# Two shared-key attentions with their q and k stacks loaded by DMA, and narrower causal scores

## The reference

```python
def _L2_xattn_ref(q, k, v):            # q = layernorm(x), k = v = ctx_512
    H, KV = 32, 8; D = E // H; G = H // KV
    qh = q.reshape(b, s, KV, G, D).transpose(0, 2, 3, 1, 4)
    kh = k.reshape(b, s, KV, D).transpose(0, 2, 1, 3)
    vh = v.reshape(b, s, KV, D).transpose(0, 2, 1, 3)
    scores = jnp.einsum('bkgsd,bktd->bkgst', qh, kh) / sqrt(D)
    weights = jax.nn.softmax(scores, axis=-1)
    out = jnp.einsum('bkgst,bktd->bkgsd', weights, vh)
x = x + _L2_xattn_ref(_layernorm(x), ctx_512, ctx_512)
```

## Time and profile before

| what | value |
|---|---|
| median of 3 runs | 4070.13 us (4068.88 to 4073.53) |
| the profiled execution | 4041.53 us |
| its span, first to last instruction | 4039.8 us |
| mean granted TensorE clock | 0.923 of full |
| PE busy | 3451.4 us (85%), 18066 instructions |
| PE weight loads | 2386.6 us (59%) |
| VectorE busy | 2419.2 us (60%) |
| ScalarE busy | 2054.4 us (51%) |
| GpSimd busy | 898.4 us (22%) |
| DMA | 346.47 MB, mean 86 GB/s |

### The profile page before, as it was taken

The page is one execution under the profiler, slowest core; times in us unless marked ns, Lnnn a source line. Parts: engine busy times, 40 slices in busy tenths (PEclk is TensorE's granted clock), DMA queues, the critical chain, the costliest instruction groups (busy, mean ns, idle before and its releaser), DMA issues. The chain is left out here.

```text
span 4039.8 us, 64864 instructions
## 1 busy us (share of the span) xinstructions
PE 3451.4 (85%) x18066; PEld 2386.6 (59%) x18070; DVE 2419.2 (60%) x4267; ACT 2054.4 (51%) x3563; POOL 898.4 (22%) x1818
## 2 busy tenths in 40 slices
PE   4349996899972799839999799899897999989998
PEld 2137775666651688714444367788775444436886
DVE  6964445455543333368888554666466788865665
ACT  5643333355531455427877633566433677774433
POOL 2410001544322100053333130122113333310000
PEclk8669998999986899959999899999998899999999
DMA  3424442400011333320000252577442000002223
GB/s 138 148 99 140 137 136 76 167 0 0 1 52 44 122 107 99 104 83 1 0 0 0 71 177 93 180 240 240 169 140 81 1 0 0 0 9 73 93 93 114
DMA packets 133100, 346.47 MB, mean 86 GB/s; under 512 B 15300, under 2 KB 15428, under 8 KB 132338
## 3 DMA queue, kind: packets, MB, share of 16 engines
q1 hardware_dynamic: 99666, 228.74, 17.5%
q0 software_dynamic: 22480, 96.23, 7.0%
q10 hardware_dynamic: 10864, 20.45, 1.4%
HBM read 274.58 MB, written 68.16 MB: 85 GB/s over the span
## 5 line engine op out<-in xcount | busy, mean ns | idle before, releaser
L1338 DVE TENSOR_REDUCE at_maxima<-psum 128x1 f32<-128x512 f32 (+1 forms) x1280 | 813.5, 661 | 288.8 <-PE psum L1148 134.8
L1309 ACT ACTIVATE at_probs<-psum 128x512 f32<-128x512 f32 (+3 forms) x1280 | 692.8, 570 | 352.1 <-PE psum L1159 200.4
L1144 PE MATMUL psum<-at_kT,at_qT 64*128 64x512 f32 (+2 forms) x1280 | 555.7, 480 | 14.9 <-DVE at_kT L1351 8.8
L1159 PE MATMUL psum<-at_qT_max,at_kT 64*128 64x512 f32 (+4 forms) x1280 | 533.0, 454 | 27.9 <-ACT at_probs L1309 23.3
L1159 PEld LDWEIGHTS psum<-at_qT_max,at_kT 64*128 64x128 f32 (+1 forms) x1280 | 218.3, 186 | 341.8 <-ACT at_probs L1309 294.6
L573 PE MATMUL psum<-f_xT_hi,ffn_w_hi 128*128 x1024 | 405.2, 396 | 9.0 <-DVE f_xT_lo L2050 2.2
L573 PE MATMUL psum<-f_xT_lo,ffn_w_hi 128*128 x1024 | 404.4, 395 | 0.0
L1176 PE MATMUL psum<-at_probs,at_vals 128*32 128x512 f32 (+4 forms) x2560 | 375.7, 578 | 2.1 <-issue 2.1
L1112 PE MATMUL psum<-ident,at_arr 128*128 128x128 f32 x1536 | 255.8, 292 | 97.2 <-POOL at_arr L1015 94.9
L1112 PEld LDWEIGHTS psum<-ident,at_arr 128*128 128x128 f32 x1536 | 169.2, 145 | 200.9 <-POOL at_arr L1015 96.2
L1003 POOL TENSOR_TENSOR at_gap<-ones 128x1 f32<-128x1 f32 x448 | 87.2, 195 | 850.3 <-DVE at_result L1365 600.0
(11 more groups left out here) (379 smaller groups left out, 7264.7 us busy)
## 6 DMA issues: line engine op xcount, KB each, us to landing
ffn_w_raw<-in_stream SPq DMA_DIRECT2D x262, 256.0 KB, 2.8
ffn_w_hi<-quantized SPq DMA_DIRECT2D x66, 512.0 KB, 3.5
ffn_w_hi<-quantized SPq DMA_DIRECT2D x65, 256.0 KB, 3.1
ffn2a_w_raw<-in_shared2a SPq DMA_DIRECT2D x26, 512.0 KB, 3.6
ffn2b_w_raw<-in_shared2b SPq DMA_DIRECT2D x26, 512.0 KB, 3.6
qz_raw<-in_stream SPq DMA_DIRECT2D x17, 768.0 KB, 4.3
quantized<-qz_quant POOLq DMA_DIRECT2D x16, 768.0 KB, 3.5
gathered<-zeros SPq DMA_DIRECT2D x1, 12288.0 KB
```

What stands on the lines that cost most here:

```text
L1144: mm = pe.matmul(bank[:, 0:width], qT[ring % 2][rows_of(h), h // HPS, t * P:(t + 1) * P], kT[ring][rows_of(h), h % 2, 0:width], start=True ...
L1159: mm = pe.matmul(bank[:, 0:S - lo], kT[ring][rows_of(h), h % 2, t * P:(t + 1) * P], qT_max[ring % 2][rows_of(h), h // HPS, lo:S], start=Tr ...
L1309: act.activation(probs[n % RING][:, 0:S - lo], scoreT[n % 2][:, 0:S - lo], ACT.Exp, scale=factor).then_inc(exped, 1)
L1338: dve.tensor_reduce(maxima[:, t, h:h + 1], (score + scoreT)[n % (4 if first else 2)][:, 0:width], AX.X, ALU.max).then_inc(maxed, 1)
```

## The change

1. The shared attentions get a stage of their own, `stage_attend_shared`. The norm now leaves the queries transposed, `xT` (high and low part, features on partitions), by its own transposes on PE into banks 4 to 7. SP spills them to DRAM (`spill`, per batch two DMAs of 1 MB), and `load` builds each group's stacks straight from DRAM: 12 DMAs, six of 64 KB for q and six of 32 KB for k. The keys' high and low parts are spilled to DRAM once, in `stage_keys_values`, by 8 DMAs of 256 KB, whose end ScalarE waits for before it reuses a buffer.
2. Groups go batch by batch (8 key heads of batch 0, then batch 1), where before batches alternated; the host's layout of `ctx_g` follows. The loop holds 8 slots now and runs 3 times.
3. The maxima go a new way: VectorE writes them to a buffer of their own (`split`), one `turn_max` after pair 5 turns them, ScalarE moves 8 rows (`maxT`), and SP puts them into the stacks by 4 DMAs (`put_max`). `turn_results` stands after pair 9. All transposes use one bank.
4. VectorE takes one maximum over two banks (two heads), 8 per group in place of 16; scores have four banks. The matmuls contract over 48 and 50 rows in place of 64.
5. POOL no longer stacks; it copies the values (`keep_values`) in place of VectorE. The clearing at the start goes from POOL to VectorE.
6. Causal scores are P (t + 1) columns wide, and their mask is always 128.

The core of the diff:

```diff
@@ stage_norm
+def stage_norm(k, nm, xT=None, tokens=None, rows=None, joined=None, beside=None, before=None, bank=0):
+            turned_ps = [room.tiles(bank + u) for u in range(TB)]
...
@@ stage_attend, scores and max_tile
-                width = min(S, P * (t + 2 - t % 2)) if causal else S
+                width = P * (t + 1) if causal else S
...
-                    m = 2 * P if t % 2 == 0 else P
-                    mm = pe.matmul(bank[:, t * P:t * P + m], ident16[:, :], mask[:, 0:m], start=False, stop=True, skip_group_check=True)
+                    mm = pe.matmul(bank[:, t * P:(t + 1) * P], ident16[:, :], mask[:, :], start=False, stop=True, skip_group_check=True)
...
@@ stage_attend_shared (new)
+    HD, H, PARTS = HEAD2, 4, 3
+    USED = PARTS * HD
+    HALF = P // 2
+    PAIRS = H * TB
+    SETS = PAIRS // 2
+    RING, SLOTS = 2 * H, 4
+    OW = P // H
+    ROUND = GROUPS // B
+    ROUNDS = (GROUPS - 1 - SLOTS) // ROUND
+    LOADS, PUTS = 2 * PARTS * 2, H
+    LAST, VALUES, MAX, RES = 1, (5, 9, 13), 5, 9
...
+        score, scoreT, res, turn = [room.psum[:, 1024 * m:1024 * m + 1024] for m in range(2)], room.banks[4:6], room.banks[6], room.tiles(7)
...
+        def head_tile(n):
+            return n // (PAIRS // 2), 1 - n % 2, n % (PAIRS // 2) // 2
...
+        @block.vector
+        def _(dve):
+            for r in range(SLOTS):
+                dve.memset(kT[r][:, :].bitcast(F32), -1.0).then_inc(cleared, 1)
+            for r in range(2):
+                dve.memset(vals[r][:, :, :], 0.0).then_inc(consts, 1)
+                dve.memset(split[r][:, :, :, :].bitcast(F32), 0.0).then_inc(consts, 1)
+            dve.wait_ge(consts, 4)
+            for r in range(2):
+                dve.memset(vals[r][:, :, HD:HD + 1], 1.0).then_inc(consts, 1)
+        made, before = queries(room, xT)
+        def spill(sp, b):
+            sp.wait_ge(made, before + TB * (b + 1))
+            part = slice(b * S, (b + 1) * S)
+            for dst, src in zip((q_hi, q_lo), xT):
+                sp.dma_start(dst.rearrange("(c p) t -> p c t", p=P)[:, :, part], src[:, :, part].bitcast(F32)).then_inc(spilled, DMA)
+        @block.sync
+        def _(sp):
+            sp.wait_ge(cleared, SLOTS)
+            def load(place, j):
+                b, n = batch_piece(place, j)
+                r, tokens = place % SLOTS, bass.ds(b * S, S)
+                for par in range(2):
+                    for i, src in enumerate((q_hi, q_lo, q_hi)):
+                        at = HALF * par + HD * i
+                        rows = src[n * H * HD:(n + 1) * H * HD, tokens].rearrange("(jj par d) t -> par d jj t", jj=2, par=2)
+                        sp.dma_start(qT[r][at:at + HD, :, :].bitcast(F32), rows[par]).then_inc(landed[r], DMA)
+                    for i, src in enumerate((k_hi, k_hi, k_lo)):
+                        at = HALF * par + HD * i
+                        sp.dma_start(kT[r][at:at + HD, :].bitcast(F32), src[n * HD:(n + 1) * HD, tokens]).then_inc(landed[r], DMA)
+            def put_max(place, j, g):
+                r = place % SLOTS
+                sp.wait_ge(max_moved, g + 1)
+                for jj in range(2):
+                    for par in range(2):
+                        at = HALF * par + USED
+                        row0 = 2 * (2 * jj + 1 - par)
+                        sp.dma_start(qT[r][at:at + 2, jj, :].bitcast(F32), maxT[place % 2][row0:row0 + 2, :]).then_inc(put[r], DMA)
+            spill(sp, 0)
+            sp.wait_ge(spilled, 2 * DMA)
+            for g in range(SLOTS - 1):
+                load(g, 0)
+            for b in range(1, B):
+                spill(sp, b)
+            put_max(0, 0, 0)
+            sp.wait_ge(spilled, 2 * B * DMA)
+            def slot(s, place, j, ahead):
+                if ahead >= 3:
+                    if not is_first(s):
+                        sp.wait_ge(scoredT, PAIRS * s)
+                    load(place + 3, j)
+                if ahead >= 1:
+                    put_max(place + 1, j, s + 1)
+            all_slots(sp, slot)
...
+            def scores(g, place, j, n):
+                jj, par, t = head_tile(n)
+                r, m = place % SLOTS, n // 2
+                if n == 0:
+                    pe.wait_ge(landed[r], LOADS * DMA * (use(place, j) + 1))
+                if n % 2 == 0:
+                    pe.wait_ge(maxed, SETS * g + m + 1)
+                mm = pe.matmul(score[m % 2][:, 512 * (n % 2):512 * (n % 2) + S], qT[r][half(par, USED), jj, t * P:(t + 1) * P],
+                               kT[r][half(par, USED), :], start=True, stop=True)
+                if n % 2 == 1:
+                    mm.then_inc(scored, 1)
+            def scores_T(g, place, j, n):
+                t, h, r = n // H, n % H, place % SLOTS
+                if n == 0:
+                    pe.wait_ge(put[r], PUTS * DMA * (use(place, j) + 1))
+                pe.wait_ge(exped, PAIRS * g + n + 1)
+                pe.matmul(scoreT[n % 2][:, :], kT[r][half(h % 2, USED + 2), t * P:(t + 1) * P], qT[r][half(h % 2, USED + 2), h // 2, :],
+                          start=True, stop=True).then_inc(scoredT, 1)
...
+            for g in range(2):
+                for n in range(PAIRS):
+                    scores(g, g, 0, n)
+                    if g == 1 and n == MAX:
+                        pe.wait_ge(made, before + N // P)
+                        turn_max(0, 0)
+            def slot(s, place, j, ahead):
+                first = is_first(s)
+                for n in range(PAIRS):
+                    scores_T(s, place, j, n)
+                    if ahead >= 2:
+                        scores(s + 2, place + 2, j, n)
+                    if n == LAST and not first:
+                        results(s - 1, place + 3, TB - 1)
+                    if n in VALUES:
+                        results(s, place, VALUES.index(n))
+                    if n == MAX and ahead >= 1:
+                        pe.wait_ge(max_moved, s + 1)
+                        if not first:
+                            pe.wait_ge(finished, s)
+                        turn_max(s + 1, place + 1)
+                    if n == RES and not first:
+                        pe.wait_ge(res_moved, s)
+                        if ahead >= 1:
+                            pe.wait_ge(max_moved, s + 2)
+                        else:
+                            pe.wait_ge(finished, s)
+                        turn_results()
...
+                for n in range(PAIRS):
+                    act.wait_ge(scoredT, PAIRS * s + n + 1)
+                    act.wait_ge(valued, PAIRS * s + n + 1)
+                    act.activation(probs[n % RING][:, :], scoreT[n % 2][:, :], ACT.Exp, scale=factor).then_inc(exped, 1)
+                    if n == LAST + 1 and not is_first(s):
+                        move_res(s - 1)
+                    if n == MAX + 1 and ahead >= 1:
+                        move_max(s + 1, place + 1, j)
...
+            def max_set(g, m):
+                jj, _, t = head_tile(2 * m)
+                dve.wait_ge(scored, SETS * g + m + 1)
+                dve.tensor_reduce(maxima[:, t, 2 * jj:2 * jj + 2], score[m % 2].rearrange("p (h s) -> p h s", h=2), AX.X, ALU.max).then_inc(maxed, 1)
...
@@ stage_keys_values
+            def batch(b, s):
+                sp.wait_ge(c_lo_made, b + 1)
+                for dst, src in ((k_hi, c_hi), (k_lo, c_lo)):
+                    sp.dma_start(dst[:, bass.ds(b * S, S)], src[s][:, :].bitcast(F32)).then_inc(kept[s], DMA)
...
+                act.wait_ge(kept[s], 2 * DMA * (uses + 1))
@@ lay_out
-        "ctx_g": np.ascontiguousarray(ctx_512.reshape(B, TB, P, 8, HEAD2).transpose(2, 3, 0, 1, 4).reshape(P, GROUPS, TB, HEAD2)),
+        "ctx_g": np.ascontiguousarray(ctx_512.reshape(B, TB, P, 8, HEAD2).transpose(2, 0, 3, 1, 4).reshape(P, GROUPS, TB, HEAD2)),
```

216 lines of the change are left out of this document (176 added, 40 removed).

## The result

| | before | changed |
|---|---|---|
| median | 4070.13 us (7 runs, 4064.8 to 4075.5) | 4081.12 us (7 runs, 4075.2 to 4090.2) |
| ratio, 95% interval | | 1.0029 (1.0017 to 1.0042) |
| span of the profiled execution | 4039.8 us | 4079.3 us |
| mean granted clock | 0.923 | 0.910 |

The change makes the kernel slower, by 0.3%. The forecast was 8.5 us faster; the time is inside its range, the direction is wrong. The page of the changed kernel: engines, then the granted clock by 40 slices.

A forecast was written before the change was run, and what follows sets the result against it. The prediction took a loop of waits between PE and ScalarE to bound the shared attentions' slots. Its terms, -14 - 8.5 + 6 + 3 + 5 = -8.5 us, applied to the median 4070.1, gave 4061.6 us, range 4022 to 4096.

The forecast's parts named there:

- What bounds the kernel: Shared attentions: a loop between PE and ScalarE sets each slot's four quarters (3.10, 3.59, 4.18, 3.69 us), not PE's sum.
- VectorE: In the slots: eight reductions of 1024 at 1.2 us each, at most 12.2 of 14.56 us, not on the path.
- The register instructions: In the shared attentions' loops: one more PE register instruction per second pair, 0.05 us each, +3 us, bounds -11 to +17.
- The causal attention: First attention, 32 slots: four tiles per slot lose 128 columns of score and mask, 0.44 us a slot, -14 us.
- the two ways in: Stretches before the first transposed score: second attention -8.5 us (-12 to -4), third attention +6 us (+2 to +10).
- The slots: Second and third attention: a slot stays 14.56 us, leaving only +3 us in the loops and +5 in the last slots.
- The last slots: End of both shared attentions, from slot 29, with fewer transposes and scores: +0.7 and +1.8 us, +5 for two layers.
- (a): Rival: PE is the bound after all, so fewer transposes shorten the slots: about 3920 or about 4000 us; chance 0.10.
- (b): Rival: the DMAs of a slot land 1 us late in each slot, +60, about 4130 us; chance 0.08.
- (c): Rival: register waits take 0.3 us a slot (+14), ways in at upper bounds (+4.5, +4): about 4084 us; chance 0.11.
- (d): Rival: matmuls of 48 and 50 rows no longer run side by side, +300, about 4370 us; chance 0.01.
- The sum: Whole kernel: -14 - 8.5 + 6 + 3 + 5 = -8.5 us, with bounds of -31 and +21.

The follow-up runs named there:

- act4: The changed kernel with ScalarE's loop of 8 slots written as one of 4 slots, the same instructions executed in the same order; ratio 1.0012 to the kernel before.
- moves_only: The changed kernel with its two ScalarE moves, move_res and move_max, one exponential later each, transposes left in place; ratio 0.9882 to the kernel before.
- place_act4: The changed kernel with turn_max after pair 3, turn_results after 11, move_res after exponential 3, and ScalarE's loop of 4 slots; 3934.6 us, ratio 0.9677.

## Why the prediction was wrong

- **What bounds the kernel: right.** "So a quarter is not PE's sum." A third of PE's transposes stayed, PE's busy time fell by 8 of 50 us, and the slot stayed at 14.5. All four quarters came out within 0.04 us, and the experiments moved three of them by the amount that the loop gives, while 3.10 stayed.
- **VectorE: right.** A reduction of 1024 takes 1.22 us (1.2 taken), and nothing waits for it in the loop.
- **The register instructions: wrong, small.** "I take 0.05 for it": a quarter at full clock lost nothing. In the loops of act4, which no pause or fall disturbs, a slot is 14.51 us against 14.56, so the +3 is -3.
- **The causal attention, the two ways in: right**, -13.4, -7.8 and +5.6 for -14, -8.5 and +6.
- **The slots: the step that failed.** "In the loops PE has one more register instruction for each second pair" is all that I let the new loops cost, with bounds from -11 to +17. Two things were missing, the jump back and the clock, both put at nothing without a reason. The loop body became 8 slots long, which the part on the change says itself; each of its two jumps back in an attention stops ScalarE for 2.0 us. And the earlier trace rows show a full clock at 49.4 of 50 us busy; I carried that clock over to a PE that is busy 41.5. The four pauses with their falls measured 14.6 us, lone falls 7.3, falls in the last slots 13.5. act4 took the first away (1.0012), and its profile has none of the second. The last are missing in the profile of moves_only, in both attentions, and in the third attention of place_act4, whose PE has the same work there. What makes the clock fall in one execution or one kernel and not in the next, in the loops and in the last slots, stays open: the pauses are shown to be the program's, the other 20.8 us are only located.
- **The last slots.** "+5" for both attentions; from pair 1 of slot 29 to the routing it is 19.8, of it 13.5 by the falls.
- **The rivals.** (a) did not happen: with the transposes gone the slot stayed. (b) did not: in a steady slot no transposed score waits for a DMA. (c) gave 4084 and the time was 4081, but for other reasons: its register waits were nil, and the ways in stayed at -7.8 and +5.6 where it had -4 and +10. (d) did not: 48 and 50 rows run side by side as 64 did. The times of (b) and (d) are added to 4070, those of (a) and (c) to the forecast's 4061.6; that changes none of these verdicts.
- **The sum.** With 36 in place of 8 for the slots the same sum is 19.5 us above before; the ratios 1.0029 and 1.0050 are 12 and 20 us.

## What to carry to other kernels

Before pricing removed work, find the loop of waits: mark a repeated burst, measure the marks where some of the work is missing already, and see whether the distance changes. What then counts is where an instruction stands, in a wait or behind the burst, more than how many there are: two numbers were worth 113 us here, sixteen transposes a slot nothing. And whoever makes a loop's body longer, or an engine more idle, adds two prices to the sum: the jump back, which is to be looked up for each engine by the length of its own body, and the clock of TensorE.
